# Row-by-row fetch of one gathered tile in 64 by SyncE, in the relational layers of a graph network

## The reference

```python
def rel_graph_conv(h, src, dst, etype, coef, bases, loopw, bias):
    hs = h[src]                                   # one row of 128 floats per edge
    c = coef[etype]
    m = c[:, 0:1] * (hs @ bases[0])
    for b in range(1, bases.shape[0]):
        m = m + c[:, b:b + 1] * (hs @ bases[b])
    agg = segment_sum(m, dst, num_segments=h.shape[0])
    return agg + h @ loopw + bias
# layers 4 and 5: msg = (x @ W[r])[rel, src]; relu(segment_sum(msg, dst) + x @ SW + b)
```

## Time and profile before

| | |
|---|---|
| median of 3 runs | 7826.15 us (7825.49 to 7827.81) |
| the profiled execution | 7854.72 us, span 7852.9 us |
| POOL busy | 5699.8 us (73% of the span) |
| PE busy | 5322.9 us (68%) |
| DVE busy | 3239.8 us (41%) |
| ACT busy | 1009.7 us (13%) |
| SP | issues DMAs only |

### The profile page before, as it was taken

One profiled execution on the slowest core, in us unless ns is written; L12 is line 12 of the kernel. 1 busy time (PEld: TensorE's weight loads), 2 busy tenths in 40 slices (PEclk: granted clock), 3 DMA queues, 4 the chain that ended last, 5 costly groups with the idle time before them and its releaser, 6 DMA issues. The chain is left out here.

```text
span 7852.9 us, 105970 instructions
## 1 busy us (share of the span) xinstructions
PE 5322.9 (68%) x25966; PEld 4714.6 (60%) x25967; DVE 3239.8 (41%) x10580; ACT 1009.7 (13%) x2622; POOL 5699.8 (73%) x6265
## 2 busy tenths in 40 slices
PE   7877777778776666677777776666666667644444
PEld 5766656677756556566666765555556556533333
DVE  5545454444445555544444662222223323312222
ACT  1111111111111111122222011111111111100000
POOL 6777767777767777677777337777767777677776
PEclk7677777766677777655555887777777777655555
DMA  3222222222222222222222642222222222212222
GB/s 109 76 74 75 73 72 71 75 75 75 76 53 53 55 55 55 58 65 65 66 65 65 189 138 52 56 55 55 56 52 54 55 55 56 53 52 56 55 55 54
DMA packets 324391, 531.22 MB, mean 68 GB/s; under 512 B 116072, under 2 KB 179733, under 8 KB 323925
## 3 DMA queue, kind: packets, MB, share of 16 engines
q0 software_dynamic: 186496, 383.17, 18.1%
q1 hardware_dynamic: 89185, 119.37, 5.3%
q10 hardware_dynamic: 48500, 26.51, 1.1%
HBM read 448.44 MB, written 80.14 MB: 67 GB/s over the span
## 5 line engine op out<-in xcount | busy, mean ns | idle before, releaser
L610 POOL DMA_INDIRECT ring<-h_table,edges_i x3328 | 3203.9, 963 | 1093.8 <-issue 1078.3
L889 PE MATMUL sum<-onehot,ring 128*128 128x128 f32 x8320 | 1747.7, 345 | 1038.3 <-DMA ring<-h_table,edges_i 831.9
L889 PEld LDWEIGHTS sum<-onehot,ring 128*128 128x128 f32 x8320 | 1390.4, 238 | 1354.8 <-DMA ring<-h_table,edges_i 979.2
L1188 DVE TENSOR_TENSOR acc<-msg,acc 128x16 f32 x4160 | 728.6, 175 | 2796.6 <-PE msg L896 2294.4
L896 PE MATMUL msg<-work,mix_w 128*128 128x128 f32 x4992 | 1080.3, 404 | 275.5 <-ACT work L689 269.3
L896 PEld LDWEIGHTS msg<-work,mix_w 128*128 128x128 f32 x4992 | 1002.0, 307 | 348.9 <-issue 336.4
L689 ACT ACTIVATE work<-sum 128x512 f32<-128x512 f32 x1040 | 620.4, 597 | 3788.7 <-PE sum L889 3720.8
L610 POOL DMA_INDIRECT ring<-in_x_dram,edges_i x832 | 814.6, 979 | 275.7 <-issue 266.2
L561 POOL DMA_INDIRECT sorted_rows<-ring,pos_i x832 | 808.1, 971 | 282.8 <-issue 247.2
L593 POOL DMA_INDIRECT ring<-h_table,pos_i x832 | 794.5, 955 | 274.8 <-issue 274.8
L896 PE MATMUL msg<-work,rel_w 128*128 128x128 f32 x3328 | 738.2, 412 | 183.8 <-ACT work L689 183.0
(11 more groups left out here) (197 smaller groups left out, 3677.3 us busy)
## 6 DMA issues: line engine op xcount, KB each, us to landing
ring<-sorted_rows SPq DMA_DIRECT2D x208, 260.0 KB, 3.1
ring<-h_table,edges_i POOLq DMA_INDIRECT x3328, 2.5
edges_i<-bucket_flat SPq DMA_DIRECT2D x208, 208.0 KB
h_table<-rows ACTq DMA_DIRECT2D x78, 256.0 KB
ring<-in_x_dram,edges_i POOLq DMA_INDIRECT x832, 2.5
ring<-h_table SPq DMA_DIRECT2D x832, 8.0 KB
sorted_rows<-ring,pos_i POOLq DMA_INDIRECT x832, 2.3
ring<-h_table,pos_i POOLq DMA_INDIRECT x832, 2.5
```

Source lines behind the costliest of these rows:

```text
L610: nc.gpsimd.indirect_dma_start(out=rows_in[:, s, :], out_offset=None, in_=rows_of[:, :], in_offset=bass.IndirectOffsetOnAxis(ap=srcT_i[:, ...
L889: last = nc.tensor.matmul(SUM[q % 2][:, t * KEYS:(t + 1) * KEYS], rows_in[:, 4 * q + t, :], onehot[:, 4 * q + t, :], start=True, stop=True)
L1188: nc.vector.tensor_tensor(acc[:, at], MSG[h][:, s * WIN:(s + 1) * WIN], acc[:, at], ALU.add).then_inc(added, 1)
```

## The change

In the relational layers the last tile (slot 15) of every fourth turn is no longer gathered by POOL: 13 tiles of 832 in a layer (`QUADS` = 13), 65 in all. SP gets them. For each group of four turns ("quad") `lend` does this:

1. It loads the 128 source numbers of the tile into `lent_i` (one partition, 512 bytes).
2. In four parts of 32 rows, it reads 8 numbers at a time into registers and issues 8 DMAs of one row (512 bytes) each, from the table into `lent`, a side buffer of 64 KB. Before the first part it waits for the list and for the copy of the quad before (`lent_placed`), which frees `lent`. In layers 0 and 1 the two bucket loads of a turn (and their waits) stand before each part.
3. It waits for all 128 rows (`lent_landed`) and for `summed[3]` of the third turn of the quad, which frees slot 15, and copies `lent` to slot 15 with one DMA.

PE waits for `lent_placed` as well before the last tile of a turn; the wait for `gathered[15]` then counts one gather less in four. In layer 0 `lend` begins where SP's bucket loop began; in the other layers it begins when the table is stored (`table_stored`). `SHORT_LAG` = 2 takes the place of `LAG` = 4 in layers 0, 1 and 4: two chunks fewer are written out, and the loop runs one round more.

```diff
+QUAD = 4
+QUADS = TURNS // QUAD
+SHORT_LAG = 2
+            def lend(l, n, p, between=None):
+                K = P * (REL_BEFORE[l] * QUADS) + p * QUADS + n
+                listed, placed, landed, free = (sp.snap(v) for v in (K * 16 + 16, K * 16 + 1, K * (16 * D) + 16 * D, K * QUAD + QUAD))
+                sp.dma_start(lent_i[:, :], src[bass.ds(n * (QUAD * RING * D) + (QUAD * RING - 1) * D, D)]
+                             .rearrange("(o e) -> o e", o=1)).then_inc(lent_in, 16)
+                for part_of in range(QUAD):
+                    if between:
+                        between(n, part_of)
+                    if part_of == 0:
+                        sp.wait_ge(lent_in, listed)
+                        apart(sp)
+                        sp.wait_ge(lent_placed, placed)
+                        apart(sp)
+                    for first in range(D // QUAD * part_of, D // QUAD * (part_of + 1), 8):
+                        _, sources = nc.values_load_multi_w_load_instructions(
+                            lent_i[0:1, first:first + 8], engines=[SP], min_val=0, max_val=N_NODES - 1,
+                            skip_runtime_bounds_check_because="sources are numbers of nodes")
+                        for e in range(8):
+                            sp.dma_start(lent[first + e:first + e + 1, :], rows_from[l][bass.ds(sources[e], 1), :])\
+                              .then_inc(lent_landed, 16)
+                sp.wait_ge(lent_landed, landed)
+                apart(sp)
+                sp.wait_ge(summed[3], free)
+                apart(sp)
+                sp.dma_start(rows_in[:, RING - 1, :], lent[:, :]).then_inc(lent_placed, 16)
...
+            for l in range(2):
+                if l:
+                    table_stored(l)
...
+                def buckets(n, part_of):
+                    i = sp.snap(n * QUAD + (l * TURNS + part_of))
+                    for h in range(2):
+                        sp.wait_ge(bucket_used[h], i + 1)
+                        load_flat(bucket_flat, bucket_of, bucket_in, h, i * HALF + HALF // 2 * h)
+
+                with sp.Fori(0, QUADS) as n:
+                    lend(l, n, more, buckets)
...
+            table_stored(2)
+            lend_passes(2, P)
...
+            for l in (4, 5):
+                table_stored(l)
+                lend_passes(l, P)
...
                             for s in range(HALF * h, HALF * (h + 1)):
+                                if s == RING - 1 and i % QUAD == QUAD - 1:
+                                    continue
                                 nc.gpsimd.indirect_dma_start(
...
-                                    pe.wait_ge(gathered[4 * q + t], i * 16 + (GATHER_PASS * r + 16))
+                                    if 4 * q + t < RING - 1:
+                                        pe.wait_ge(gathered[4 * q + t], i * 16 + (GATHER_PASS * r + 16))
+                                    else:
+                                        pe.wait_ge(gathered[4 * q + t], gathers_there)
+                                        pe.wait_ge(lent_placed, lent_there)
```

More of the change, by code:

```diff
@@ L114, in edge_passes, with edge_chunks @@
                 moved(p)
-def edge_chunks(nc, eng, P, more, before, turn, round_end, step, last):
+def edge_chunks(nc, eng, P, more, before, turn, round_end, step, last, lag):
     def rounds(c):
@@ L128, in rounds @@
         return end
-    for c in range(LAG):
+    for c in range(lag):
         step(c, c % 2, c // 2, rounds(c))
-    with eng.Fori(LAG // 2, CHUNKS // 2) as n:
+    with eng.Fori(lag // 2, CHUNKS // 2) as n:
         for j in range(2):
@@ L416, in count, with gathers @@
             return P * (layers_before * TURNS) + p * TURNS + i
+        rows_from = [x] + [tables[(l - 1) % 2] for l in range(1, len(LAYERS))]
+        def gathers(s):
+            return GATHER_PASS - 16 * QUADS if s == RING - 1 else GATHER_PASS
         def apart(eng):
@@ L443, in _, with lend_passes, table_stored @@
                 sp.dma_start(xT[:, c * CHUNK:c_end * CHUNK], x_cols[:, c * CHUNK:c_end * CHUNK]).then_inc(x_in[n], 16)
+            sp.wait_ge(passes_set, 1)
+            P = sp.value_load(passes[0:1, 0:1], min_val=1, max_val=MAX_PASSES)
+            more = sp.value_load(passes[0:1, 1:2], min_val=0, max_val=MAX_PASSES - 1)
+            def lend(l, n, p, between=None):
[23 more added lines that the diff above has]
+                sp.dma_start(rows_in[:, RING - 1, :], lent[:, :]).then_inc(lent_placed, 16)
+            def lend_passes(l, p_end):
+                with sp.Fori(0, p_end) as p:
+                    with sp.Fori(0, QUADS) as n:
+                        lend(l, n, p)
+            def table_stored(l):
+                for j in range(2):
+                    sp.wait_ge(rows_dma[j], 16 * dma_before(l, j) + 16)
+            with sp.If(more > 0):
+                lend_passes(0, more)
             sp.wait_ge(key_set, 1)
@@ L617, in _ @@
                         for h in range(2):
-                            pool.inc_swdge_sem(gathered[HALF * h:HALF * (h + 1)], [GATHER_PASS] * HALF, mode="sub")
+                            pool.inc_swdge_sem(gathered[HALF * h:HALF * (h + 1)], [gathers(s) for s in range(HALF * h, HALF * (h + 1))],
+                                               mode="sub")
         @block.scalar
@@ L1015, in _ @@
                     edge_chunks(nc, pe, P, more, r, messages_ranking if r < 2 else messages, round_end, rel_step,
-                                CHUNKS + 3 if layer["norm"] else CHUNKS + 1)
+                                CHUNKS + 3 if layer["norm"] else CHUNKS + 1, LAG if layer["norm"] else SHORT_LAG)
                 else:
@@ L1550, in _ @@
                     edge_chunks(nc, dve, P, more, r, turn_ranking if r < 2 else turn_settling if r == 2 else turn, round_end,
-                                rel_step, CHUNKS + 2 if layer["norm"] else CHUNKS + 1)
+                                rel_step, CHUNKS + 2 if layer["norm"] else CHUNKS + 1, LAG if layer["norm"] else SHORT_LAG)
                 else:
```

20 lines of the change are left out of this document (12 added, 8 removed).

## The result

The changed kernel takes 7753.26 us (median of 4 runs, 7748.31 to 7756.65), beside 7825.82 for the kernel before: ratio 0.9903, interval 0.9891 to 0.9914. It is 73 us **faster**; I had forecast 36 us slower, and my range began at 7772. On a second chip it was 7749.7 against 7826.8, ratio 0.9901 (0.9884 to 0.9917).

The account below looks back on a forecast made before the run. POOL's issue bounds the kernel now; SP's round of 64.0 + 10.6 + 2.4 + 1.0 + 2.0 = 80.0 us would exceed POOL's 79.4 and become the bound. Layers: 47 + 19 - 14 - 16 = +36, so 7826 + 36 = 7862 us; range 7772 to 8020.

Parts of the forecast that it names:

- What bounds the kernel: All five relational layers: POOL's rate of issue sets their length, 1.260 to 1.291 us a tile; PE follows.
- 128 row DMAs at 0.50 us: SP's round: one-row DMAs priced like layer 3's 16-row ones, 64.0 us; ends 0.48 and 0.77 us each.
- 16 register loads at 0.66: SP's round: loads of row numbers into registers, 0.53 of each the instruction, 10.6 us in all.
- The rest: SP's round: list and copy DMAs 0.5 us each; loop end, register instructions and waits 2.0 us (ends 1 and 3.5).
- The sum: SP's round in layers 2, 4 and 5: 80.0 us, above POOL's 79.4, so SP becomes the bound.
- Layer 1: Bucket loads add 3.9 us, making SP's round 83.9 us; the layer goes from 1072.7 to 1091.9 us, +19.
- Layer 0: SP gets to its bucket loads only at 49.9 us, a lateness never made good; rounds of 83.9 us, +47 us.
- Who waits for a late SP: Relational layers: the ring catches a late copy once (8 tiles, some 10 us), then POOL goes at SP's pace, 13 rounds.
- the threshold at 79.4 us: SP's round: the sign of the change turns at about 79.4 us, POOL's time for 63 tiles.
- Hidden work: Bucket loads queued behind 32 rows (19 us) and PE's register instructions cost nothing; without cover, up to 2 us a turn.
- The first rival: SP's round is 77 us (80.9 in layers 0 and 1), POOL stays the bound: -58 us, 7768; chance 0.20.
- the third: Rival: one-partition DMAs cost what ACT's did, 0.68 to 0.77 us: +1500 us; chance of dearer still 0.11.

Follow-up runs that it names:

- skipping kernel: Changed kernel with SP's list load, row fetches and copy and PE's wait for the copy left out, so nobody fetches the 65 tiles: 7744.0 us, ratio 0.9891.

## Why the prediction was wrong

- **What bounds the kernel** was right: POOL's rate of issue. Without 65 gathers it is 83 us shorter, as I had written.
- **128 row DMAs at 0.50 us**: wrong, and this is the step that failed. I took the price from the 16-partition DMAs because those of 16, 104 and 128 partitions cost the same 313 to 320 ns, and concluded that size doesn't matter. It costs 225 ns, 0.408 from start to start: 128 x 0.092 = 11.8 us less. The ends I gave, 0.48 and 0.77, didn't hold it; the lower end should have gone to well below the nearest row, as no row had a single partition on SP. The row that seemed to bear on it (ACT's 586 ns) pointed the wrong way.
- **16 register loads at 0.66**: too low. The instruction takes 782 ns instead of 526, and a load adds 0.82 us to a step: in layers 2, 4 and 5 a step with a load in it is 1.24 us in the mean, one without 0.422 (median 0.408). So the loads cost 16 x 0.16 = 2.6 us more than I had, and single longer steps 128 x 0.014 = 1.8. The row of the timeline agrees: 112 x 0.422 + 15 x 1.24 = 65.9, beside 65.8 from the first row's start to the last one's.
- **The rest**: from the copy to the first row 5.9 us and from the last row to the next copy 1.9, together 7.9. One row (0.42) and one load (0.82) are in it, so the rest is 6.6, where I had 2.4 + 1.0 + 2.0 = 5.4: 1.2 more. The wait for the last row, of which I had put 1.2 in, is 1.1 (55.3 / 52).
- **The sum**: 80.0 - 11.8 + 2.6 + 1.8 + 1.2 = 73.8; the trace has 73.7 in the first round of layer 2 and 73.4 in the mean without the waits for PE. So SP is not the bound in layers 2, 4 and 5, and each saves what 13 gathers cost: 17.5 to 18.4 us beside the kernel before on the same chip (I had -14, -8, -8).
- **Layer 1**: SP's own round is 77.7 us, not 83.9. Copies are 80.7 apart in the mean, as SP waits 3 us a round for DVE. The bucket loads cost 77.7 - 73.4 = 4.3 us a round, where I had 3.9. First to last gather is 1052.4 instead of 1070.2, -18 where I had +19.
- **Layer 0**: +47 was forecast, -10 came (-7 on the second chip). SP starts 30 us late as I said (first rows at 51). But its own round is 77.6 us, below POOL's 63 gathers (63 x 1.29 = 81.3), so it makes up in each round part of what it was late: PE waits for the first three copies (22.6 us in all), SP waits for DVE only after its sixth copy, and its last copy is at 1071.9, before POOL's last gather at 1081.9. "SP has no slack left" hung on the same term. The 5.87 us that I put down to SP's late start now aren't its doing: that wait ends at 45.74, before SP's first bucket load at 50.1, and the skipping kernel has one of 4.8 us at the same place.
- **Who waits for a late SP, the threshold at 79.4 us, 13 rounds a layer**: borne out by the kernels with 16 and 32 more rows, at both sides of it, within the 78.8 to 83.9 that they leave open.
- **Hidden work** (PE's registers, the bucket loads behind 32 rows) cost nothing that can be measured. But the bucket loads aren't hidden at the start of layer 0: DVE waits 20 us for the first four, instead of 4 before. POOL didn't wait for it.
- The first rival was the right one (POOL stays the bound), and I gave it 0.20 at -58 us. Its reasons (shorter landings, quick register work) were not: the landings were as I had them, the register loads dearer, and the row DMA cheaper. It was 15 us short, mostly since I had even its layer 0 at +8. Its own number, 7768, lay outside my range, which began at 7772: a case with a chance of 0.20 should have been in it. Of the signs, SP's waits for PE spoke for this rival, while the DMA instruction was far from 316 ns as in the third, but to the cheap side, for which I had no case.

The direction turned on a difference of 0.6 us between two sums of 80, one of which had an unmeasured term taken 128 times. The range was drawn as if that term were known to 5%.

## What to carry to other kernels

Where a change stands or falls with a small price that is paid a hundred times a round, the range has to span the whole of what that price can be, below the nearest row too; a kernel with 16 or 32 more DMAs a round shows such a margin at once. Work given to a second engine is free up to its own round and then costs the full difference each time, so the margin between the two rounds (here 5 to 6 us of 79, and 3 in layer 1) is a number to state with the gain. That margin is the other engine's own work against the pace of the first; the distance of its copies hides it, as its waits are in it. The same change lost 14% (10561.8 against 9296.1) on a chip where the sequencers ran slower: here the long stream of tiny sequencer instructions was more sensitive to that than the gathers that it replaced.

## What the runs showed of the hardware

- A DMA issued by SP costs its sequencer 225 ns for one partition, 253 for 4, 277 for 8, 303 for 12, 321 for 16; 17 rows cost as little as 1 (247 and 252 ns), and 106 rows less than 96 (279 and 361). The Trainium skill ("DMA: Bandwidth & Descriptors", Why a DMA increments its semaphore by 16 and not by 1) says that a DMA's data goes to the largest number of engines up to 16 that divides the slowest dimension of both its sides evenly, so that 127 partitions use one. The packets of 4 bytes agree with it to the last one: 9425 more in the kernel after than in the kernel before, which is 1 for each of 8320 rows and 65 lists and 16 for each of 65 copies. The price agrees only in the main (104 rows cost more than 96); the Trainium skill gives none.
- A register load of 8 values took 526 ns from `window` and 782 from `lent_i`. The Trainium skill ("DMA: Bandwidth & Descriptors", Latency and other measured facts) has a floor of about 600 ns: one is below it and one well above.
- The copy from the side buffer to the ring, SBUF to SBUF over 128 partitions, takes 508 ns to issue, against 320 for the 260 KB loads from DRAM over as many partitions.
- On three chips a register instruction of 37 ns in the median lasted up to 1.4 us, and on the chip with 9296 us a step between two row DMAs took 0.79 us in the mean instead of 0.422; the kernel before took 9296 to 9401 us on them instead of 7826.
